# FFN0 gate logits with the tokens on the output partitions, in a two-layer attention and FFN kernel on one core

## The reference

```python
logits = jnp.einsum('bsh,he->bse', hidden_states, gate_w)      # 512 channels -> 8 experts
routing_weights, selected_experts = jax.lax.top_k(logits, K)   # K = 2
h = jax.nn.relu(jnp.einsum('bsh,hi->bsi', hidden_states, up_w)) ** 2
shared_out = jnp.einsum('bsi,ih->bsh', h, down_w)
x_latent = jnp.einsum('bsh,hl->bsl', hidden_states, fc1_w)     # 512 -> 256
expert_out = jnp.einsum('bsl,lm->bsm', x_latent, expert_w)     # 256 -> 256
moe_out = expert_out * jnp.sum(routing_weights, axis=-1, keepdims=True)
routed_out = jnp.einsum('bsl,lh->bsh', moe_out, fc2_w)         # 256 -> 512
return _layernorm(shared_out + routed_out, ln_gamma, ln_beta)
```

## Time and profile before

| | us |
|---|---|
| three timed runs | 1267.16, 1273.1, 5874.38 |
| median of the three | 1273.1 |
| span of the profiled execution | 1270.4 |
| TensorE busy in it | 1179.2 (93%) |
| VectorE, ScalarE, GpSimd busy | 646.5, 506.6, 369.8 |

### The profile page before, as it was taken

How to read it: one execution, slowest core, us unless ns; L and a number is a source line. 1 busy time by engine, 2 the same in 40 slices (tenths; PEclk the granted TensorE clock), 3 DMA queues, 4 the chain that set the end, 5 groups by cost and what they waited for, 6 DMA issues and landing times.

```text
span 1270.4 us, 15419 instructions
## 1 busy us (share of the span) xinstructions
PE 1179.2 (93%) x5582; PEld 926.3 (73%) x5582; DVE 646.5 (51%) x1107; ACT 506.6 (40%) x1369; POOL 369.8 (29%) x249
## 2 busy tenths in 40 slices
PE   5989998998998999987898998989989899898998
PEld 3766776776776678865777887878878788787774
DVE  5364356357248733377634625446254462544764
ACT  4354265246147523423533515335153351533530
POOL 3142043024024174455412404224042240322340
PEclk9999999999999999998999998999999999999997
DMA  7010010000000121100110101001010010100001
GB/s 242 1 38 25 1 37 25 0 25 25 0 18 1 47 91 61 51 34 1 50 34 33 50 0 50 33 33 50 0 50 33 33 50 0 36 33 1 4 8 67
DMA packets 10325, 43.43 MB, mean 34 GB/s; under 512 B 1300, under 2 KB 1556, under 8 KB 7604
## 3 DMA queue, kind: packets, MB, share of 16 engines
q1 hardware_dynamic: 10292, 42.99, 9.7%
HBM read 40.89 MB, written 2.10 MB: 34 GB/s over the span
## 4 chain that ended last, share of the span: by engine, by line
PE 73%; DVE 15%; ACT 6%; issue 4%; POOL 2%; DMA 0%; DVEq 0%; ACTq 0%; POOLq 0%
PE work L435 13%; PE work L436 13%; PE work L437 13%; PE work L496 5%; DVE neg_max L1289 5%; PE yb L435 4%; PE yb L437 3%; PE yb L436 3%; DVE neg_max_raw L1286 3%; ACT prob L919 3%; PE ov L435 3%; PE ov L437 2%; PE pt L435 2%; PE ov L436 2%; PE pt L437 2%
## 5 line engine op out<-in xcount | busy, mean ns | idle before, releaser
L1089 POOL TENSOR_TENSOR prob<-prob,exp_rcp 128x512 f32<-128x512 f32 (+1 forms) x96 | 127.2, 1325 | 698.3 <-DVE exp_rcp L1263 698.3
L919 ACT ACTIVATE prob<-work,neg_max 128x128 f32<-128x128 f32 (+1 forms) x384 | 149.3, 402 | 149.3 <-DVE neg_max L1289 149.1
L435 PE MATMUL work<-xT_hi,q_hi 128*128 128x512 f32 (+1 forms) x448 | 186.7, 417 | 4.8 <-DVE xT_lo L1352 4.8
L436 PE MATMUL work<-xT_lo,q_hi 128*128 128x512 f32 (+1 forms) x448 | 181.4, 405 | 0.0
L437 PE MATMUL work<-xT_hi,q_lo 128*128 128x512 f32 (+1 forms) x448 | 180.9, 404 | 0.0
L496 PE MATMUL work<-kT,qT 128*128 128x128 f32 (+1 forms) x768 | 128.1, 309 | 1.1 <-DVE qT L1201 0.9
L496 PEld LDWEIGHTS work<-kT,qT 128*128 128x128 f32 (+1 forms) x768 | 114.0, 190 | 13.9 <-issue 1.7
L871 ACT ACTIVATE pT_hi<-pt 128x512 fp32r<-128x512 f32 x128 | 73.5, 600 | 117.6 <-PE pt L506 117.4
L1320 DVE TENSOR_TENSOR oT_lo<-ov,oT_hi 32x128 fp32r<-32x128 f32 (+2 forms) x160 | 67.1, 420 | 89.1 <-ACT oT_hi L877 87.8
L435 PE MATMUL yb<-o_hi,oT_hi 128*128 128x512 f32 x224 | 94.2, 421 | 14.8 <-DVE oT_lo L1320 14.8
L435 PEld LDWEIGHTS work<-xT_hi,q_hi 128*128 128x128 f32 (+1 forms) x448 | 84.5, 189 | 28.0 <-DVE xT_lo L1352 5.5
(11 more groups left out here) (182 smaller groups left out, 2196.0 us busy)
## 6 DMA issues: line engine op xcount, KB each, us to landing
q_raw<-in_l_q SPq DMA_DIRECT2D x8, 1024.0 KB, 4.8
o_raw<-in_l_o SPq DMA_DIRECT2D x8, 1024.0 KB, 4.8
kv_raw<-in_l_kv SPq DMA_DIRECT2D x8, 515.0 KB, 3.3
q_raw<-in_l_q SPq DMA_DIRECT2D x4, 768.0 KB, 4.4
o_raw<-in_l_o SPq DMA_DIRECT2D x4, 768.0 KB, 4.2
qT<-in_ctxT SPq DMA_DIRECT2D x4, 512.0 KB, 6.9
x<-in_x SPq DMA_DIRECT2D x2, 1024.0 KB, 12.2
q_raw<-in_up SPq DMA_DIRECT2D x2, 1024.0 KB, 6.2
```

What stands on the lines that cost most here:

```text
L435: pe.matmul(dst, l_hi, r_hi, start=first and k == 0, stop=False)
L436: pe.matmul(dst, l_hi, r_lo, start=False, stop=False)
L919: e = act.activation(prob[:, i % 2, g * L.keys:(g + 1) * L.keys], s[:, g, :], ACT.Exp, bias=neg_max[:, i % 2, g:g + 1], scale=L.scale, acc ...
L1089: pool.tensor_tensor(p, p, exp_rcp[:, b % 2, :].unsqueeze(2).broadcast_to([P, G, L.keys]), ALU.mult)\
```

## The change

The gate product is made with the operands exchanged: blocks of 128 tokens of `xT` are stationary (128 columns) and the gate weights move (8 columns). The logits of block b come out with the tokens on the partitions, at the place in `pt` where the transposes had put them. The copy on VectorE, the eight transposes on TensorE and the semaphore between them go. VectorE waits for the one remaining gate signal.

```diff
             def gate(half):
 
                 pe.wait_ge(f0.gate_split_lo, 1)
-                return product(pt[0:NE, half, :], [((gate_hi[:, k, :], gate_lo[:, k, :]), xt)
-                                                   for k, xt in enumerate(columns(xT_hi, xT_lo, half * HALF, HALF))])
+                for b in range(4 * half, 4 * half + 4):
+                    mm = product(pt[:, 0, b * NE:(b + 1) * NE],
+                                 [(xt, (gate_hi[:, k, :], gate_lo[:, k, :]))
+                                  for k, xt in enumerate(columns(xT_hi, xT_lo, b * P, P))])
+                return mm
...
             gate(1).then_inc(f0.gate, 1)
             expert(1)
-
-            pe.wait_ge(f0.gate_copied, 1)
-            for b in range(NB):
-                mm = pe.transpose(pt[:, 0, b * NE:(b + 1) * NE], logitsT[0:NE, b * P:(b + 1) * P], ident[0:NE, 0:NE])
-            mm.then_inc(f0.gate, 1)
...
-            dve.wait_ge(f0.gate, 1)
-            dve.tensor_copy(logitsT[0:NE, :], pt[0:NE, :, :].rearrange("p a t -> p (a t)")).then_inc(f0.gate_copied, 1)
             lin_lo(6)
             lin_lo(7)
 
-            dve.wait_ge(f0.gate, 2)
+            dve.wait_ge(f0.gate, 1)
```

More of the change, by code:

```diff
@@ L170, in __init__ @@
         self.gate = sem(f"{prefix}_gate")
-        self.gate_copied = sem(f"{prefix}_gate_copied")
         self.route_top = sem(f"{prefix}_route_top")
@@ L308, in build_program @@
         y2 = [yb, ov]
-        logitsT = relu[:, :, :].rearrange("p a t -> p (a t)")
         d2 = [ov[:, :], pt[:, 1, :]]
```

## The result

The changed kernel takes 1279.09 us (median of 14 runs, 1271.39 to 1285.05), the kernel before 1267.06 (median of 14). The ratio is 1.0118, with a 95% interval of 1.0086 to 1.015. The forecast was 1281.3. The medians differ by 12.0 us, which is less than the 2% bound for a verdict, and the interval lies clear of 1. The quotient of the two medians is 1.0095, inside the interval; why the ratio on record lies above it, the runs do not show. The profiled execution of after took 1277.37 us and has a span of 1275.5, so 1.87 us lie around the span.

A forecast was written before the change was run, and what follows sets the result against it. TensorE, busy 93% of the span, was taken as the bound. Gate +5.5, wait -0.2, transposes -0.1 and clock +5.7 gave +10.9 on 1270.4, so 1281.3 us; whole range 1271 to 1288.

The forecast's parts named there:

- The gate's pace: In both gate halves: 48 products at 0.115 us, 5.52 us in place of 2.78, both halves 5.5 us more.
- The choice between L806 and L728: Nearest trace row for the gate's pace: 0.12 us a product with 16 moving columns, or 0.065 from the transposes; former preferred.
- The transposes: After `expert(1)`: TensorE gains 0.68 us, but the third down product waits 0.6; net gain 0.1, bounds 0 and 0.68.
- the limit that I had named as proof of the contrary: Forecast wrong if time between `expert(1)` and the third down product falls by more than 0.3 us.
- The wait ahead of `expert(0)`: After `gate(0)` and block 6's transposes: 0.19 us idle for an `fc1` tile's low part goes; 0.2 us credited.
- Sum without the clock: Gate +5.5, less 0.2 for the wait and 0.1 for the transposes: +5.2 us.
- The clock: Falls to 0.50 in each gate half for 6.8 us, costing 6.3, less 0.6 for absorbed waits: +5.7 us.
- The waits of 0.21 and 0.36: TensorE waits tied to the transposes of blocks 6 and 7; absorbed in the low clock stretches, 0.6 us credited.
- The base: Whole kernel: forecast starts from the profiled span, 1270.4 us, adding nothing for what lies around it.
- The clock holds: Rival for the gate halves: weight loads and small products keep the clock up; +5.2 us, 1275.6 us; chance 0.31.
- not slower: Rival on gate pace: 0.065 us or less, weight loads running beside earlier products; +0.4, 1270.8 us; chance 0.09.
- down throughout: Rival: clock falls in `gate(0)` and stays down past `gate(1)`; about +35 us, so 1305; chance 0.04.

The follow-up runs named there:

- e2_wide: Changed kernel with each gate product streaming 128 columns, not 8; 1277.78 us, ratio 1.0033 to the kernel before, stage 35.00 us.
- e3_no_transposes: Kernel before without the VectorE copy and the eight transposes, gate otherwise as it was; 1273.27 us, ratio 1.0, stage 30.23 us.
- e1_spread: Changed kernel with gate block 0 ahead of `expert(0)` and the other seven between products of 512 columns; 1280.81 us, ratio 1.0057, stage 37.94 us.
- e7_pack_tokens: Changed kernel with high and low gate weights side by side: 16 moving columns, 32 products in a half; 1278.03 us, ratio 1.0036.
- e8_again: Changed kernel, no edit, measured again on another set's chip; ratio 1.0026 to the kernel before, median of all 12 runs 1280.48 us.
- e5_spread2: Changed kernel with gate blocks 0 and 1 at the head, the others among full products; 1275.16 us, ratio 1.0028, stage 35.09 us.
- the second set: The unedited changed kernel measured again (e8_again): median 1280.48 us beside 1273.15 for the kernel before.
- e4_pack: Kernel before with high and low gate weights side by side as 16 stationary columns, 16 products not 24; 1273.83 us, ratio 0.9998.

## Why the prediction was right

The pieces of the stage, each from one start to the next on TensorE, in us. The column without the clock's fall is e2_wide.

| piece | before | clock held | after |
|---|---|---|---|
| `gate(0)` | 2.78 | 5.31 | 5.73 |
| transposes, `expert(0)`, `fc1` | 10.10 | 9.96 | 12.03 |
| `gate(1)` | 2.78 | 5.30 | 6.37 |
| `expert(1)` and, in before, transposes | 3.47 | 2.85 | 4.94 |
| first to third down product | 2.87 | 3.25 | 3.25 |
| third down to first `up` product | 8.25 | 8.33 | 8.33 |
| sum | 30.25 | 35.00 | 40.65 |

- **The gate's pace.** Taken at 0.115 us a product, measured 0.112; a half is 5.3 and not 5.52. The two halves add 2.53 + 2.52 = 5.05 us, where 5.5 was forecast. The choice between L806 and L728 as the nearest row was right. The Trainium skill (TensorE: Matmul & The Clock Gate, LDWEIGHTS) gives a weight load as columns / 1.2 ns, an estimated 107 ns for 128 columns whatever the number of rows; at the full clock the 0.112 here (128 rows) and the 0.12 of L806 (40 rows) agree, and the 0.065 of L728 (8 rows) does not the earlier trace rows. At a granted clock of 0.50 the pace was 0.21, about twice that figure.
- **The transposes.** Their 0.62 us (3.47 - 2.85) went, 0.38 of it came back ahead of the third down product, which waited 0.34 for `acc` and not the 0.6 forecast, and 0.08 just behind it. That is 0.16 net, where I took 0.1; in e3_no_transposes nothing was left of it. The moment of the third down product, counted from the last product of `expert(1)`, moved from 3.78 to 3.48 in after. I had forecast that it stays, and this 0.3 stands right at the limit that I had named as proof of the contrary. Of it 0.17 is a shorter step on VectorE (1.08 from the top 8 to the scaling before, 0.91 after, because adding up `route` took 0.34 and then 0.17). The other 0.13 is the way from the scaling's start to the product (1.03 before, 0.90 after): in before the product followed the one ahead of it at the usual pace, so it had this much room, which I had overlooked. In e3_no_transposes, also without the transposes, the step on VectorE stays at 1.11 and the moment is 3.69. Why `route` is faster in after, the runs do not show.
- **The wait ahead of `expert(0)`.** A credit of 0.2 was forecast. From the transposes to `expert(0)` it took 0.58 us before and 0.38 with the clock held, but later waits took part of this back, and the whole piece behind `gate(0)` is 0.14 shorter. Sum without the clock: 5.05 - 0.14 - 0.16 = +4.75, forecast +5.2.
- **The clock.** It fell in each half, for 6.8 us each time, as taken. The cost is the difference of the last two columns, 5.65 (0.42, 2.07, 1.07 and 2.09 by pieces), forecast 5.7. The waits of 0.21 and 0.36 went, as forecast: the only wait of over 0.1 us that the trace of after names in the stage is the 0.34 for `acc`. That both stretches had just the length that was taken is in part luck: the runs show 3.4 us (e1_spread, e7_pack_tokens), 6.8, and in the second profile of the changed kernel 6.8 and 10.2.
- **The clock outside the profiles.** Every run lists its mean granted clock. It averages 0.973 over the 14 runs of the changed kernel and over the 12 of e8_again, 0.976 over the 60 runs of before on the chips of the experiments, 0.9755 over the 6 of e2_wide and 0.9756 over the 12 of e5_spread2. So the fall is not of one profile alone. The difference from the last two, about 0.003 of some 1277 us, is by an estimate 7 to 8 us at the lower clock (0.003 x 1277 / 0.5 = 7.7), where the profile has 13.6. So the 5.65 holds for the profiled execution; the mean over the runs may be little more than half of it.
- **The sum.** Stage +10.40, forecast +10.9. The difference of the medians is 12.0, and in the second set 7.3. What lies between these and the stage, the runs do not settle.
- **The base.** I added nothing for what lies around the span; after has 1.87 us there. The profiled before was then 3.3 us above the median of 14 (1270.4 against 1267.06) even so. So the base was 3.3 too high and the change, +10.9 against the 12.0 of the medians, 1.1 too low. The two partly cancel: that 1281.3 lies only 2.2 from 1279.09 is in part luck.
- **The rivals.** "The clock holds" is refuted by the stretches, "not slower" by the pace, "down throughout" by the 1.00 from 452 to 460.

Not tried: other widths of the moving operand, and weight loads with no product behind them. Why the length of the low stretches differs between two executions stays open.

## What to carry to other kernels

Count a product with few moving columns at the price of its weight load, not of its columns: here 0.11 us, so exchanging the operands to be rid of 8 transposes bought 64 more instructions at a loss. Look at the granted clock of a stretch even where TensorE is 100% busy; put full products between runs of small ones where the order allows it. Before an instruction is taken off the busiest engine, find the next wait behind it: three of these experiments (e1_spread, e3_no_transposes, e4_pack) gained on TensorE and lost it to VectorE's `h_lo` or `acc`.

## What the runs showed of the hardware that was not expected

- The pace is the same for 8 and for 128 moving columns (0.11 us), at a clock of 1.00; but 48 products on end of 8 columns lost the clock (0.50 for 6.8 us behind each half), and those of 128 did not (1.00 from 436 to 474). With 24 of 8 columns on end it held in e5_spread2.
- In e1_spread the clock fell after a wait of 1.46 us behind 12 small products and four transposes (0.56 in 442 to 444), while e4_pack, with products of 512 columns there, waited 0.91 us at the same place and kept it (1.00), as before does with waits of up to 0.36 us.
- In e7_pack_tokens two halves with the same products behaved differently: 0.50 for 3.4 us behind the first, 1.00 in the second.
- Two profiles of one kernel have low stretches of different length at the same place (6.8 and 10.2 us), and the 796 to 803 us behind the stage, which the change does not touch, scatter by nearly 7 us from one execution to the next.
